# Cross-attention on one core: TensorE's work within an attention step in another order, with one visit of four mixes and the denominators' products by themselves

## What is computed

```python
q = hidden_state @ Wq + bq
k = encoder_hidden_state @ Wk + bk
v = encoder_hidden_state @ Wv + bv
q = q.reshape(b, l, KVH, GROUPS, HD).transpose(0, 2, 3, 1, 4)
k = k.reshape(b, s, KVH, HD).transpose(0, 2, 1, 3)
v = v.reshape(b, s, KVH, HD).transpose(0, 2, 1, 3)
scores = jnp.einsum('bkgld,bksd->bkgls', q, k) * scale
scores = scores + encoder_attention_mask[:, :, None, :, :]
attn = jax.nn.softmax(scores, axis=-1)
out = jnp.einsum('bkgls,bksd->bkgld', attn, v)
out = out.transpose(0, 3, 1, 2, 4).reshape(b, l, H)
x = out @ Wo + bo + hidden_state
mu, var = mean(x), var(x)
return (x - mu) * rsqrt(var + EPS) * gamma + beta
```

## Time and profile before

| | before |
|---|---|
| median of 3 runs | 3776.23 us (3775.29 to 3780.36) |
| the profiled execution | 3775.84 us, its span 3774.2 us |
| mean granted TensorE clock | 0.989 |
| PE busy | 3732.4 us (99%) |
| GpSimd busy | 2888.1 us (77%) |
| VectorE busy | 2526.6 us (67%) |
| ACT busy | 1993.1 us (53%) |

### The profile page before, as it was taken

One profiled execution on the slowest core, in us unless ns is written; L12 is line 12 of the kernel. 1 busy time (PEld: TensorE's weight loads), 2 busy tenths in 40 slices (PEclk: granted clock), 3 DMA queues, 4 the chain that ended last, 5 costly groups with the idle time before them and its releaser, 6 DMA issues. The chain is left out here.

```text
span 3774.2 us, 53803 instructions
## 1 busy us (share of the span) xinstructions
PE 3732.4 (99%) x20274; PEld 2380.4 (63%) x20274; DVE 2526.6 (67%) x2919; ACT 1993.1 (53%) x3865; POOL 2888.1 (77%) x1101
## 2 busy tenths in 40 slices
PE   8999999999999999999999999999999999999999
PEld 7999888655555555555555555555555555547887
DVE  4444444387777777777777777777777777735676
ACT  2222222146666666676666666666666666661111
POOL 1111111259999999999999999999999999994565
PEclk9999999979999999999999999999999999999999
DMA  5545567337677677676676677677767767677774
GB/s 204 204 178 204 185 235 242 111 72 152 145 158 151 143 159 149 147 156 149 148 155 150 146 154 152 147 152 151 153 147 156 152 142 162 153 173 210 195 199 135
DMA packets 297275, 611.14 MB, mean 162 GB/s; under 512 B 132064, under 2 KB 169056, under 8 KB 264512
## 3 DMA queue, kind: packets, MB, share of 16 engines
q0 software_dynamic: 57760, 335.98, 39.7%
q1 hardware_dynamic: 236000, 265.54, 26.0%
q10 hardware_dynamic: 3264, 6.29, 0.4%
HBM read 243.98 MB, written 96.35 MB: 90 GB/s over the span
## 5 line engine op out<-in xcount | busy, mean ns | idle before, releaser
L1057 DVE TENSOR_REDUCE half_max<-score 128x1 f32<-128x800 f32 (+1 forms) x2048 | 1923.4, 987 | 652.7 <-PE score L912 643.0
L832 POOL TENSOR_TENSOR sum_pool<-sum_pool,weights 128x2048 f32<-128x2048 f32 x446 | 2142.6, 4804 | 30.9 <-ACT weights L1116 3.0
L1116 ACT ACTIVATE weights<-logit 128x512 f32<-128x512 f32 (+1 forms) x3328 | 1700.5, 611 | 704.7 <-PE logit L957 652.0
L957 PE MATMUL logit<-qk_store 98*128 98x512 f32 (+1 forms) x3328 | 1186.0, 424 | 4.2 <-ACT weights L1116 2.0
L912 PE MATMUL score<-qk_store 96*128 96x400 f32 (+1 forms) x4096 | 1150.2, 368 | 11.8 <-issue 8.2
L912 PEld LDWEIGHTS score<-qk_store 96*128 96x128 f32 x4096 | 717.9, 191 | 391.6 <-DVE half_max L1057 200.2
L957 PEld LDWEIGHTS logit<-qk_store 98*128 98x128 f32 (+1 forms) x3328 | 607.1, 185 | 399.6 <-ACT weights L1116 262.0
L967 PE MATMUL mixed<-weights,v_sb 128*32 128x512 f32 x6656 | 823.2, 602 | 0.0
L967 PEld LDWEIGHTS mixed<-weights,v_sb 128*32 128x32 f32 x6656 | 170.9, 109 | 361.8 <-issue 282.0
L832 POOL TENSOR_TENSOR sum_pool<-weights 128x2048 f32<-128x2048 f32 x64 | 294.7, 4605 | 62.1 <-ACT weights L1116 61.1
L548 POOL DMA_DIRECT2D q_parts<-mask_store x128 | 68.6, 540 | 301.5 <-DVE mask_store L501 154.5
(11 more groups left out here) (88 smaller groups left out, 2596.5 us busy)
## 6 DMA issues: line engine op xcount, KB each, us to landing
weights<-weights POOLq DMA_DIRECT2D x191, 1024.0 KB, 7.9
sum_pool<-weights POOLq DMA_DIRECT2D x63, 1024.0 KB, 7.0
qk_store<-q_parts SPq DMA_DIRECT2D x192, 256.0 KB, 3.9
qk_store<-k_parts SPq DMA_DIRECT2D x192, 200.1 KB, 7.1
q_parts<-mask_store POOLq DMA_DIRECT2D x128, 256.0 KB, 2.6
mask_store<-in_mask_Bx1xSxS_ff SPq DMA_DIRECT2D x32, 800.5 KB, 7.6
rows<-in_ctx SPq DMA_DIRECT2D x24, 1024.0 KB, 5.2
rows<-in_x SPq DMA_DIRECT2D x16, 1024.0 KB, 5.8
```

The source lines that it names most:

```text
L832: nc.gpsimd.tensor_tensor(sum_pool[s % 2][0:w], first[0:w], weights[buffer(s, st)][0:w], ALU.add).then_inc(pool_added, 1)
L957: last = nc.tensor.matmul(bank[0:w, :], k_sb[s][:, keys], q_sb[s][:, h, :], start=True, stop=not masked, skip_group_check=masked)
L1057: nc.vector.tensor_reduce(half_max[m // NROW % 2][:, k % G, k // G, j:j + 1], score[j][:, :, 0:HALVES[j][2]], mybir.AxisListType.XY, ALU.m ...
L1116: nc.scalar.activation(weights[buffer(s, st)][0:w, h, :], logit[u % BANKS][0:w, :], ACT.Exp).then_inc(exp_done, 1)
```

## The change

Two constants of `attend` change. `ORDER` has the same letters in the same numbers (52 L, 32 S, 13 M, a T and a P), in another order. As all queues that follow the string (PE's, ACT's) are built from it, ACT's work goes along; SyncE's, GpSimd's and VectorE's queues keep their order, but `LO_AT` moves VectorE's `copy_lo` from ahead of its 23rd reduction to ahead of its 25th.

```diff
-    ORDER = "LLSSMLSLLSLLSLLSLSLLSLLSLLSLMMMSSLLLMSLLSLLSLLSLLSLSLLSLLSLLSLLSTMMSLLLSLSMMMLSLLSMPMSLLLSLSLLSLLSM"
+    ORDER = "LSSLMLSLLSLLSLLSLSLLSLLSLLSMMMLSLLSLLSLLSLLSLLSLLSLSLLSLLSLLSLLSMMMMSTSMMLSLLSLLSLLSLMMLSSPLLSLSLML"
     FIRST_MIX = 1
     FIRST_LEAD = 2
     FIRST_ORDER = ORDER.replace("S", "SS", 2 * (LEAD - FIRST_LEAD))
-    LO_AT = 22
+    LO_AT = 24
```

## The result

The changed kernel takes 3927.77 us (median of 4 runs, 3918.47 to 3943.09) against 3775.76 (4 runs) before: 1.040 times the time, 95% interval 1.038 to 1.042. The profiled execution took 3935.34 us, its span 3933.7. The direction was forecast and the first cause too; the time lies 58 us above the forecast of 3870 and 8 us above the upper end of the range of 3838 to 3920.

The account below looks back on a forecast made before the run. PE was taken to bound the attention step, with ACT (VectorE close behind) pacing its two long stretches and GpSimd nearly a second bound. 3775.84 + 81 + 12 + 1 = 3870 us; eight in ten: 3838 to 3920.

Parts of the forecast that it names:

- The size of the wait: At each attention step's start the first L waits 1.3 us for the shift rows; P to first L about 5.5.
- The quiet landing: Shift rows' DMA at a step's end: in the quiet case the second row lands at P + 5.2 us.
- The term of 81: First L's wait for the shift rows, 1.3 us at each of 62 step boundaries: 81 us, bounds 62 and 105.
- The 0.1 in it for the semaphore: In the first L's wait, 0.1 us added after the shift rows' landing, taken as P + 5.4.
- The prices of the stretches: PE's work between visits of mixes, priced by items or ACT's pace: together 27.83 us a step, 27.71 before.
- the open load: After the wait at the step's start a weight load stands open: +0.1 us a step.
- the term of 12: New order of stretches and visits plus the open load: +0.2 us a step, 12 us, bounds -0.3 to +0.5 a step.
- the two waits said to be hidden: ACT idling about 1 us before logits 37 and 38, and VectorE's low-part copy two reductions later: each costs nothing.
- The clock: Rival: clock falls at step starts; 54 us more in half the steps (3924), 108 in all (3978); chance 0.18.
- The price of a fall: In the clock rival, 3.5 us at half speed around a step's start: up to 1.75 us a fall.
- the margin (1.9 us): Before the change, shift rows land about P + 5.2 and the next step's first L starts at P + 7.15.

Follow-up runs that it names:

- late_p: The kernel before with P taken out of MPM and put by itself later in the step, one visit more: 3907.09 us, ratio 1.0347.
- shift_first: Shift rows issued ahead of SyncE's wait for the denominators, in the changed kernel (3775.29 us) and in the kernel before (3778.17 us).
- shift_first_after: The changed kernel with the shift rows issued ahead of SyncE's wait for the denominators: 3775.29 us, ratio to before 0.9998.
- fill: The changed kernel with five more 128x512 products, results overwritten, ahead of each step's first L: 3886.68 us, ratio 1.0301.

## Why the prediction was wrong

**What was right.** The cause: the shift rows hang behind P through SyncE's program order, and what lies between P and the first L is less than that chain. `late_p` and both `shift_first` kernels show it from both sides. The size of the wait: P to the first L was put at 5.5 and measured 5.58 (5.28 median). The quiet landing came sooner than in the earlier trace rows, at P + 4.9, but the tail was longer than the earlier trace rows let expect, up to P + 12.9 (one landing of 8.8 from its issue). That the mean is near 5.5 all the same is in part luck. The term of 81 was 89, as the chain took 5.58 for 5.5 and the work beside it 4.14 for 4.22. The 0.1 in it for the semaphore had no row behind it; on average the first L starts 0.04 behind the landing. The prices of the stretches: 11.08 for the run of 22 L and 12 S (10.98), 7.18 (7.18), 3.80 (3.83), 3.57 for four mixes (3.57). Summed, the new order is neutral where I had +0.1, and with the open load, +0.1 as forecast, the term of 12 was 7 - 2 = 5. And the two waits said to be hidden, ACT's before logit 37 and the later low part, cost nothing: `shift_first_after` has both.

**The step that failed.** The sum has no term for the clock: it takes the idleness at each step's start to leave the clock at full. The runs show 21 falls in the 61 steady steps, which cost 65 us. With 89 for the wait and 5 for the order that is the 159 us by which the profiled spans differ, and `fill`, with most of the falls gone, takes 41 us off the median.

The clock stood among the rivals with 0.18, and was priced at 1.75 us in half of the steps, 54 us, which made 3924; the measured time is 3927.8. What made me hold it for unlikely was "the idle is followed by a mix, and the clock is at its full 2.4 GHz in the steady steps now". The second half is no evidence: in those steps PE never idles, so they say nothing of a step with 1.3 us of idleness in it. The only rows that bore on an idle PE were the earlier trace rows, and there the clock had fallen, after a gap of only 0.30 and a stretch at ACT's pace. They deserved the larger chance, and the range should have reached the rival's far end.

The Trainium skill (TensorE: Matmul & The Clock Gate, section "HAM oscillation") tells of a loop whose matmuls wait for a DMA each round and fall to the lower clock each round, but there the wait is longer than the round's work. Here the wait is 1.4 us on average, in steps of about 42, and a fall comes in about one round of three, so the page does not settle this case.

**The price of a fall** was low as well: I took one stretch of 3.5 us at half speed, as in the earlier trace rows. Here they last 6.8 us or more and cost 3.1 us each on average; the step at 1733.61 lost 4.1 us by one of 10. The old profile had a fall of that length too, in the last step (the one in the earlier trace rows lies across that step's start):

```profile
3378.50:3385.40 6.90, 6.90 (x23) 2.29 (x22) 0.00 (x0) 3.28 (x8) 6.76 (x4) 0.51 1.03 208
```

There are fewer falls than the half of the steps that the rival assumed. The two errors nearly cancel, 65 us for 54, so it is luck that its 3924 lies so near the measured time.

**What stays open.** Why `late_p`, with nearly the same waits, has ten falls and after twenty-one. At the slow landings they hardly differ: 10 of 12 such steps have a fall in `late_p`, 13 of 14 in after. The difference is in the ordinary steps, with none of 49 in `late_p` and 8 of 47 in after (slow is P + 5.9 or more, as above). In `late_p` the wait stands right behind the mix, in after one logit later, and the stretch ahead of the mix has a score more; no run tells these apart from how the steps fall in time. After's runs spread over 25 us, before's over 6. The mean granted clock of each run goes with its time: 0.974 in the one of 3918.47, 0.972, 0.969 and 0.966 in the one of 3943.09, so the time at the lower clock differs from run to run. `LO_AT` was not tried alone in the old order: with 24 there VectorE would wait for a score behind a logit that waits for VectorE.

## What to carry to other kernels

Before moving a piece of work in a hand-written order, follow its result through every queue in program order to the last thing queued behind its wait: here a product that nobody in the step needs held up two unrelated rows, and the margin (1.9 us) could be read in the old profile. When a move makes TensorE idle for about a microsecond each round, give the lower clock behind it a term and a wide range; here it added 41 (what `fill` took off) to 65 us (by the stretches). And issue first what the next round needs: `shift` moved ahead in SyncE's queue is worth 4% in this order and nothing in the old one, yet takes the trap away from both.

## What the runs showed that I had not expected

Five idle products of 128x512 a step make the kernel 1% faster, by keeping the clock up. And a lone visit can be worth its price: MM and P by themselves cost 0.14 us more than MPM, but the letters on both sides of P then take 3.03 us instead of 3.65, as P gives VectorE a pause.
